# Dense attention regrouped: heads on 32 rows each, four matrix products in different tiles, PSUM split between row maxima and exponentials

## The chip, the cores and the metric

The kernel runs on one core of a Trainium2 chip. The metric is device time in microseconds (us) of one execution; a profile of one execution of the kernel before is at hand.

## The reference, cut to what matters

The program is a chain of twelve sublayers on x, 4 batches of 512 tokens of 128 numbers, float32. Two of the twelve are the dense attentions that the change is about; both have 16 heads of 8 numbers and attend over the 512 tokens of a batch.

```python
# second sublayer ("mqa"): causal, one key and one value head for all 16 query heads
latent = x @ Wc_down                      # 128 -> 64
q = (latent @ Wq_up).reshape(B, T, 16, 8)
k, v = split(latent @ Wkv_up)             # 8 and 8
att = softmax(where(causal, einsum('bthd,bsd->bhts', q, k) / sqrt(8), -inf))
x = x + einsum('bhts,bsd->bthd', att, v).reshape(B, T, 128) @ Wc_proj

# fifth sublayer ("rope"): not causal, own keys and values in each head
q, k, v = proj(Wq, bq), proj(Wk, bk), proj(Wv, bv)      # 16 heads of 8
q, k = apply_rope(q) / sqrt(8), apply_rope(k)
x = x + (softmax(q @ k.T) @ v) @ Wo.T + bo
```

The input of each is the layer-normed x. The order is moe, mqa, moe, chan, rope, chan, swiglu, forget, swiglu, deep, time, deep. The two "deep" sublayers (six layers of windowed attention and feed-forward each) fill the last two thirds of the time and are changed only in where one set of their weights lies.

## The kernel before, in words

Tokens lie along the free dimension and the 128 features on the partitions. Each engine has its own straight program (TensorE, VectorE, ScalarE, GpSimd, and SyncE for loads); they meet by semaphores. A sublayer other than the deep ones runs as a loop over the four batches, and a batch (a "unit") begins on TensorE only when the unit before has added its result to x (`unit_done`, L411 ff.). PSUM has eight banks of 128 x 512 float32.

One unit of dense attention (`dense_pe`, `dense_act`, `dense_dve`):

- Preparation: layer norm (L145, L151, L159 on TensorE, L170 and L174 on ScalarE, L182 to L191 on VectorE), then q, k and v products (L414 to L428), rope on VectorE (L532 to L544), the values laid out (L551, L553).
- L556: VectorE makes 16 masked copies of the keys, `da_kM`, one for each head: all rows but the 8 of that head are zero, so that a product over all 128 rows gives one head's scores. Before the first unit of a sublayer, L511 clears 8320 columns for the values, which are laid out in the same manner, 128 wide with zeros and ones.
- Scores for the maxima: for each tile of 128 queries and each group of 4 heads, four products of 128 x 512 (L444; in the causal sublayer 128 to 512 keys, and one bf16 product L447 that adds the mask) fill four banks; VectorE takes the four row maxima in one reduction (L564). Eight banks hold two such groups.
- L452 turns the 64 columns of maxima, L500 on ScalarE puts them into spare rows of `da_q`, so that the second score product comes out less its maximum.
- Exponentials: for each tile of 128 keys and each head one product (L463, mask L466) into one of four banks, ScalarE takes exp (L506), and a product with the values (L473) adds into bank 6 or 7, which in the end holds both the sums and the denominators.
- End: VectorE copies and inverts the denominators (L569, L571), multiplies (L574), TensorE projects (L477), VectorE adds to x (L578 or L580).

Every matrix product here has float32 operands. In the trace one such product is two records of MATMUL and two of LDWEIGHTS; a bf16 product is one of each.

The chip's tiles can be seen in this kernel in the deep sublayers. L859 makes its four products with 64 columns of weights each, alternately into PSUM rows 0 to 63 and 64 to 127. L797 takes operands from rows 0 to 63 or 64 to 127 and writes PSUM rows in blocks of 32, eight different places in turn; L792, ahead of it, uses all rows and columns.

## Time and profile before

| what | us |
|---|---|
| median of three runs (range) | 6653.96 (6646.73 to 6661.31) |
| the profiled execution, its own time | 6652.98 |
| its span, first to last instruction | 6651.2 |
| mqa sublayer, from one sublayer's last addition to x to its own last | 646.0 |
| rope sublayer, likewise | 832.8 |

The profile page gives busy time by engine over the whole span, and a strip of forty slices; each digit is tenths of full. As the program is a chain of sublayers with different limits, an average over the whole says little about two of them. The two dense sublayers are read as stretches of their own. A TensorE record's length holds the way through the array too, so that consecutive records overlap: the spacing of their starts is what a stream costs, not their length.

### The profile page before, as it was taken

How to read it: one execution, taken by the hardware profiler on the slowest of the kernel's cores; microseconds unless marked ns; L12 is line 12 of the kernel's file. 1: busy time of each engine (PE TensorE's matmuls, PEld its weight loads, DVE VectorE, ACT ScalarE, POOL GpSimd, SP SyncE). 2: the span in 40 equal slices, each digit the busy share in tenths (PEclk: the TensorE clock that was granted, in tenths of full speed). 3: DMA queues.
4: the chain of work that ended last, by engine and by line, in shares of the span. 5: the costliest groups of instructions: out<-in, count | busy, mean ns of one | idle time of the engine just before them, and what ended most of it. 6: DMA issues, size and time to landing. Idle time of an engine off the chain costs nothing.

```text
span 6651.2 us, 145048 instructions
## 1 busy us (share of the span) xinstructions
PE 5355.9 (81%) x64980; PEld 3035.4 (46%) x64980; DVE 3759.9 (57%) x4061; ACT 2357.0 (35%) x2740; POOL 2981.6 (45%) x1264
## 2 busy tenths in 40 slices
PE   5888868898964678888888888856888888888887
PEld 2455533343432344554555545423455555545454
DVE  4222343321224377777777777645777777777774
ACT  1222221122232344444444444423444444444443
POOL 0000000000000277777777777506777777777773
PEclk8888868999965689999999999967998999999998
DMA  1000000000000011111110111100101111111110
GB/s 64 1 0 0 0 0 0 0 0 0 0 0 0 3 26 26 42 26 42 26 42 23 42 26 26 26 34 13 29 23 42 26 42 26 40 26 42 26 26 23
DMA packets 77764, 142.42 MB, mean 21 GB/s; under 512 B 18632, under 2 KB 25488, under 8 KB 75536
## 3 DMA queue, kind: packets, MB, share of 16 engines
q1 hardware_dynamic: 77200, 133.84, 7.8%
q8 instruction: 483, 7.91, 0.5%
q14 instruction: 81, 0.66, 0.0%
HBM read 38.36 MB, written 1.05 MB: 6 GB/s over the span
## 4 chain that ended last, share of the span: by engine, by line
PE 64%; DVE 16%; ACT 7%; issue 7%; POOL 5%; SPq 0%; DVEq 0%; DMA 0%; POOLq 0%; ACTq 0%
PE psum L828 11%; PE psum L444 6%; PE psum L463 6%; PE psum L473 6%; PE psum L890 5%; PE psum L797 4%; PE psum L878 4%; PE psum L859 4%; DVE arena L1093 3%; ACT arena L983 3%; PE psum L811 3%; PE psum L845 3%; DVE arena L1106 2%; DVE arena L1102 2%; POOL arena L1206 2%
## 5 line engine op out<-in xcount | busy, mean ns | idle before, releaser
L1206 POOL TENSOR_TENSOR arena<-arena,minus_half 128x16 f32<-128x16 f32 x384 | 1125.0, 2930 | 1034.0 <-DVE arena L1095 1031.7
L828 PE MATMUL psum<-deep_wqkv,arena 128*128 128x512 f32 x1536 | 877.8, 701 | 432.2 <-DVE arena L1106 424.2
L1221 POOL MEMSET arena<- 128x33 f32 x4 | 0.4, 128 | 2432.0 <-DVE std L1425 2432.0
L1208 POOL TENSOR_TENSOR arena<-arena 128x1024 f32<-128x1024 f32 x384 | 903.4, 2353 | 0.0
L1211 POOL TENSOR_TENSOR arena<-arena 128x1024 f32<-128x1024 f32 x384 | 889.5, 2316 | 30.1
L983 ACT ACTIVATE arena<-psum 128x1024 f32<-128x1024 f32 x384 | 393.4, 1024 | 1040.1 <-PE psum L828 1040.0
L1093 DVE TENSOR_REDUCE arena<-arena 128x16 f32<-128x1024 f32 x384 | 467.0, 1216 | 448.2 <-ACT arena L983 446.6
L828 PEld LDWEIGHTS psum<-deep_wqkv,arena 128*128 128x128 f32 x1536 | 300.8, 212 | 792.2 <-DVE arena L1106 518.7
L845 PEld LDWEIGHTS psum<-w_ident,arena 128*128 128x128 f32 x3072 | 398.7, 153 | 254.9 <-issue 250.6
L1085 DVE TENSOR_TENSOR arena<-arena 128x1024 f32<-128x1024 f32 x192 | 491.8, 2561 | 6.6
L1102 DVE TENSOR_TENSOR arena<-psum,arena 128x1024 f32<-128x1024 f32 x384 | 467.2, 1217 | 0.0
L1106 DVE TENSOR_TENSOR arena<-psum,arena 128x1024 f32<-128x1024 f32 x384 | 465.8, 1213 | 0.0
L463 PE MATMUL psum<-arena 128*128 128x512 f32 (+3 forms) x1024 | 455.5, 529 | 10.4 <-ACT arena L500 10.4
L569 DVE COPY arena<-psum 64x512 f32<-64x512 f32 x16 | 11.0, 689 | 784.0 <-PE psum L473 783.8
L473 PE MATMUL psum<-arena 128*128 128x512 f32 (+3 forms) x1024 | 453.2, 527 | 0.0
L444 PE MATMUL psum<-arena 128*128 128x512 f32 (+3 forms) x1024 | 409.9, 550 | 40.7 <-DVE arena L556 37.2
L845 PE MATMUL psum<-w_ident,arena 128*128 128x128 f32 x3072 | 433.5, 288 | 2.4 <-ACT arena L1000 2.4
L506 ACT ACTIVATE arena<-psum 128x512 f32<-128x512 f32 (+3 forms) x512 | 264.9, 517 | 477.3 <-PE psum L463 281.6
L1071 DVE TENSOR_REDUCE arena<-psum 128x16 f32<-128x1024 f32 x192 | 235.1, 1225 | 336.5 <-PE psum L797 336.5
L989 ACT ACTIVATE arena<-psum 128x1024 f32<-128x1024 f32 x384 | 392.0, 1021 | 82.5 <-PE psum L845 82.4
L878 PEld LDWEIGHTS psum<-arena 64*64 64x64 f32 x24576 | 380.5, 136 | 61.0 <-issue 60.4
L878 PE MATMUL psum<-arena 64*64 64x32 f32 x24576 | 402.2, 221 | 2.7 <-issue 2.7
(247 smaller groups left out, 8031.5 us busy)
## 6 DMA issues: line engine op xcount, KB each, us to landing
arena<-arena SPq DMA_DIRECT2D x672, 128.0 KB, 2.4
deep_wqkv<-in_deep_wqkv SPq DMA_DIRECT2D x12, 1536.0 KB, 7.0
deep_wo<-in_deep_wo SPq DMA_DIRECT2D x12, 512.0 KB, 7.5
arena<-arena SPq DMA_DIRECT2D x96, 64.0 KB, 2.0
deep_w<-in_deep_w SPq DMA_DIRECT2D x12, 341.0 KB, 7.6
deep_w<-in_deep_w SPq DMA_DIRECT2D x12, 192.0 KB, 7.5
deep_scales<-in_deep_scales SPq DMA_DIRECT2D x12, 128.0 KB, 8.1
x<-in_x SPq DMA_DIRECT2D x4, 256.0 KB, 3.4
```

The source lines that it names most:

```text
L444: last = nc.tensor.matmul(bank(a + j)[:, 0:keys], da_q[:, h // HALF, qt * P:(qt + 1) * P], da_kM[:, h, 0:keys], start=True, stop=not causal)
L463: last = nc.tensor.matmul(a[:, q0:T], da_kM[:, h, kt * P:(kt + 1) * P], da_q[:, h // HALF, q0:T], start=True, stop=not causal)
L473: nc.tensor.matmul(bank(6 + h // HALF)[:, q0:T], da_Vm[:, h, kt, :], da_PT[:, v % BUFS, q0:T], start=(kt == 0 and h % HALF == 0), stop=(kt ...
L828: last = nc.tensor.matmul(bank(2 + cc), xs[unit_ % 2][:, WIN + t * P:WIN + (t + 1) * P], wqkv[:, half * INNER + cc * 512:half * INNER + (c ...
L845: last = nc.tensor.matmul(turns[:, m * P:(m + 1) * P], roped[:, h:h + 2, :], w.ident[:, :], start=True, stop=True, is_transpose=True)
L878: last = nc.tensor.matmul(bank(odd)[64 * side:64 * side + 64, to:to + WIN], V[64 * r:64 * r + 64, WPT * t + jj, (pair + odd) * 64:(pair + ...
L1093: nc.vector.tensor_reduce(h_sum[a % 2][:, hs], qk_sq[:, hs, :], AX.X, ALU.add).then_inc(de.deep_sq_summed, 1)
L1102: nc.vector.tensor_tensor(turned[:, hs, :].rearrange("p h (a e) -> p h a e", a=2), swapped, sin, ALU.mult).then_inc(de.deep_rope_parts, 1)
L1106: nc.vector.tensor_tensor(roped[:, hs, :], qk_half, under(tabs[:, 2 * half, t, :], shape), ALU.mult).then_inc(de.deep_rope_parts, 1)
L1206: nc.gpsimd.tensor_tensor(h_inv[a % 2][:, hs], h_sum[a % 2][:, hs], minus_half[:, :], ALU.pow).then_inc(de.deep_inv_ready, 1)
L1208: nc.gpsimd.tensor_tensor(dst[:, hs, :], dst[:, hs, :], turned[:, hs, :], ALU.add).then_inc(de.deep_summed, 1)
L1211: nc.gpsimd.tensor_tensor(dst[:, hs, :], dst[:, hs, :], over(h_inv[a % 2][:, hs], [P, LHEADS, LD]), ALU.mult).then_inc(de.deep_roped, 1)
```

## The change: what it does

Both dense sublayers are written anew.

- A head has 32 rows instead of 8 of 128: row 0 to 7 its numbers, row 8 a one in the keys and (later) minus the maximum in the queries, the rest zero. Four heads make a set, four sets a batch. The widening is made by products with fixed 0/1 matrices (`ra_widen`, four for q and four for k in each batch) or with padded weights (`mqa_q`, `mqa_k`); ScalarE copies each result out. The values are 32 wide with a one at column 8, so that their product gives the denominator in row 8. The masked key copies, the clearing of the value area and the two-half layout go.
- The preparation of all four batches comes first, one batch's layer norm beside the one before; then all score work; then all ends. The per-batch loop is gone: the instructions are written out.
- Score products take 32 rows, the four heads of a set on four different row blocks. The products for the maxima go one head at a time into three single banks (0 to 2) and VectorE reduces each by itself. The products for the exponentials go two heads at a time into a pair of banks (3 and 4, or 5 and 6), and ScalarE takes exp of a pair in one instruction. The value products write 32 rows of bank 7 each, four heads side by side; ScalarE copies bank 7 out after the four key tiles of a set.
- In one step TensorE issues for one tile: a maxima product, two exponential products, a maxima product, the same again, and then the value products of the tile before. The maxima are those of batch b and the exponentials those of batch b - 1, in five rounds; the first has no exponentials and the last no maxima. The maxima are turned once for each set, and VectorE adds them into `da_Q`.
- At the end of a sublayer each batch has eight products of 128 x 512 with fixed matrices (`dense_sum_pe`), which gather the sums and the denominators from the widened rows, then a reciprocal, a product, the projection (`dense_out_pe`) and the addition to x.
- The second set of deep weights moves into the arena, over space that the dense sublayers use, and its first load waits until the first deep sublayer begins. The loads at the start lose those 2.6 MB and gain some 1.2 MB of wider matrices.

The added code, cut to its core (preparation, bias, rope and end functions left out):

```diff
--- before.py
+++ after.py
-ARENA = 34400
-EARLY = 20700
+ARENA = 39860
+ODD_LAYER = 34430
+EARLY = 30724
...
-        deep_kept = [{n: sb(f"{n}_{h}", list(d[n].shape[1:])) for n in layered} for h in range(2)]
-        deep_w = [namedtuple("Layer", [n[5:] for n in layered])(*deep_kept[h].values()) for h in range(2)]
...
+        top[0] = ODD_LAYER
+        deep_kept = [{n: sb(n + "_0", list(d[n].shape[1:])) for n in layered}, {n: new(*d[n].shape[2:]) for n in layered}]
+        deep_w = [namedtuple("Layer", [n[5:] for n in layered])(*deep_kept[h].values()) for h in range(2)]
...
+        SETS = 4
+        GROUPS = SETS * TILES
+        KEY_ORDER = (2, 3, 0, 1)
+        WIDE = SETS * P
+        da_Q = new(NB * SETS, T)
+        da_K = new(NB * SETS, T)
+        da_V = new(NB * TILES, WIDE)
+        da_PT = new(2 * SETS, T)
+        mx = new(SETS * TILES, P)
...
+        def bank_use(q, x_, j):
+            return (17 * q - 1 if q else 0) + 4 * x_ + j + (1 if q and x_ else 0)
+        def bank_use_max(q):
+            return 17 * (q + 1) - 1 + (4 if q + 1 < NB * SETS else 0)
...
+        def dense_wide_pe(pe, e, lhs, src, N):
+            if e >= 2:
+                pe.wait_ge(da.wide_kept, N.wide_kept + e - 1)
+            nc.tensor.matmul(bank(4 + e % 2), lhs, src, start=True, stop=True).then_inc(da.wide_ready, 1)
+        def dense_scores_pe(pe, causal, b, s, x_, j, N):
+            v, keys = bank_use(b * SETS + s, x_, j), (x_ + 1) * P if causal else T
+            if v >= 3:
+                pe.wait_ge(da.banks_free, N.banks_free + v - 2)
+            apart(pe)
+            r32, to = slice(32 * j, 32 * j + 32), bank(v % 3)
+            last = nc.tensor.matmul(to[:, 0:keys], da_Q[r32, b * SETS + s, x_ * P:(x_ + 1) * P],
+                                    keys_of(causal, b, s)[r32, 0:keys], start=True, stop=not causal)
             if causal:
+                last = nc.tensor.matmul(to[:, x_ * P:keys], identb[:, :], later_key_q[:, :], start=False, stop=True)
+            last.then_inc(da.scores_ready, 1)
+        def dense_max_pe(pe, q, N):
+            v = bank_use_max(q)
+            pe.wait_ge(da.banks_free, N.banks_free + max(v - 2, bank_use(q, TILES - 1, 3) + 1))
+            for qt in range(TILES):
+                last = nc.tensor.matmul(bank(v % 3)[:, qt * P:(qt + 1) * P], mx[:, q % SETS * TILES + qt, :], w.ident[:, :],
+                                        start=True, stop=True)
+            last.then_inc(da.max_turned, 1)
+        def dense_keys_pe(pe, causal, b, s, kt, half, N):
+            group = GROUPS * b + TILES * s + kt
+            q0 = kt * P if causal else 0
+            kk = keys_of(causal, b, s)
+            m = 2 * group + half
+            if kt == 0 and half == 0:
+                pe.wait_ge(da.banks_free, N.banks_free + bank_use_max(b * SETS + s) + 1)
+            if m >= 2:
+                pe.wait_ge(da.probs_ready, N.probs_ready + m - 1)
+            apart(pe)
+            for at in range(2):
+                j = KEY_ORDER[2 * half + at]
+                r32, to = slice(32 * j, 32 * j + 32), bank(3 + 2 * (m % 2) + at)
+                last = nc.tensor.matmul(to[:, q0:T], kk[r32, kt * P:(kt + 1) * P], da_Q[r32, b * SETS + s, q0:T],
+                                        start=True, stop=not causal)
+            if causal:
+                for at in range(2):
+                    last = nc.tensor.matmul(bank(3 + 2 * (m % 2) + at)[:, q0:q0 + P], identb[:, :], later_key_k[:, :], start=False,
+                                            stop=True)
+            last.then_inc(da.keys_ready, 1)
+        def dense_mix_pe(pe, causal, group, N):
+            b, s, kt = group // GROUPS, group // TILES % SETS, group % TILES
+            q0 = kt * P if causal else 0
+            pe.wait_ge(da.probs_ready, N.probs_ready + 2 * group + 2)
+            if kt == 0 and group >= TILES:
+                pe.wait_ge(da.y_kept, N.y_kept + group // TILES)
+            apart(pe)
+            for at in range(SETS):
+                j = KEY_ORDER[at]
+                c0 = 0 if causal else s * P + 32 * j
+                last = nc.tensor.matmul(bank(7)[32 * j:32 * j + 32, q0:T], da_V[:, b * TILES + kt, c0:c0 + 32],
+                                        da_PT[:, group % 2 * SETS + at, q0:T], start=(kt == 0), stop=(kt == TILES - 1),
+                                        skip_group_check=True)
+            last.then_inc(da.pv_done, 1)
+        def dense_attend_pe(pe, causal, N):
+            made = 5 * NB if causal else 8 * NB
+            pe.wait_ge(da.wide_kept, N.wide_kept + made)
+            pe.wait_ge(da.v_kept, N.v_kept + (NB if causal else NB * TILES))
+            for body in range(NB + 1):
+                for s in range(SETS):
+                    for x_ in range(TILES):
+                        group = GROUPS * (body - 1) + TILES * s + x_
+                        for half in range(2):
+                            if body < NB:
+                                dense_scores_pe(pe, causal, body, s, x_, 2 * half, N)
+                            if body >= 1:
+                                dense_keys_pe(pe, causal, body - 1, s, x_, half, N)
+                            if body < NB:
+                                dense_scores_pe(pe, causal, body, s, x_, 2 * half + 1, N)
+                        q = body * SETS + s - 1
+                        if x_ == 0 and 0 <= q < NB * SETS:
+                            dense_max_pe(pe, q, N)
+                        if group >= 1:
+                            dense_mix_pe(pe, causal, group - 1, N)
+            dense_mix_pe(pe, causal, GROUPS * NB - 1, N)
+        def dense_sum_pe(pe, b, N):
+            pe.wait_ge(da.y_kept, N.y_kept + SETS * (b + 1))
+            if b >= 2:
+                pe.wait_ge(da.y_ready, N.y_ready + b - 1)
+            for to, lhs, done in ((2 * (b % 2), w.da_den, da.den_ready), (2 * (b % 2) + 1, w.da_own, da.ysum_ready)):
+                for s in range(SETS):
+                    last = nc.tensor.matmul(bank(to), lhs[:, s, :], da_Q[:, b * SETS + s, :], start=(s == 0), stop=(s == SETS - 1))
+                last.then_inc(done, 1)
+        def dense_exp_act(act, causal, group, N):
+            q0 = group % TILES * P if causal else 0
+            for half in range(2):
+                m = 2 * group + half
+                if half == 0 and group >= 2:
+                    act.wait_ge(da.pv_done, N.pv_done + group - 1)
+                act.wait_ge(da.keys_ready, N.keys_ready + m + 1)
+                at = group % 2 * SETS + 2 * half
+                nc.scalar.activation(da_PT[:, at:at + 2, q0:T], banks(3 + 2 * (m % 2), 2)[:, :, q0:T],
+                                     ACT.Exp).then_inc(da.probs_ready, 1)
+        def dense_y_act(act, q, N):
+            act.wait_ge(da.pv_done, N.pv_done + TILES * (q + 1))
+            nc.scalar.activation(da_Q[:, q, :], bank(7), ACT.Copy).then_inc(da.y_kept, 1)
+        def dense_max_dve(dve, causal, b, s, x_, j, N):
+            q = b * SETS + s
+            v, keys = bank_use(q, x_, j), (x_ + 1) * P if causal else T
+            dve.wait_ge(da.scores_ready, N.scores_ready + 4 * (TILES * q + x_) + j + 1)
+            if x_ == 0 and j == 0 and q >= SETS:
+                dve.wait_ge(da.max_turned, N.max_turned + q - SETS + 1)
+            at = 32 * j + HD8
+            nc.vector.tensor_reduce(mx[:, s * TILES + x_, at:at + 1], bank(v % 3)[:, 0:keys], AX.X, ALU.max,
+                                    negate=True).then_inc(da.banks_free, 1)
+        def dense_lay_max_dve(dve, q, N):
+            v = bank_use_max(q)
+            dve.wait_ge(da.max_turned, N.max_turned + q + 1)
+            nc.vector.tensor_tensor(da_Q[:, q, :], bank(v % 3), da_Q[:, q, :], ALU.add).then_inc(da.banks_free, 1)
...
                     load_layer(sp, c, 0)
+                    sp.wait_ge(g.unit_done, first_deep)
                     load_layer(sp, c, 1)
...
-                    per_unit(pe, dense_pe, u, n, k, kind == "mqa", other)
+                    dense_pe(pe, u, n, kind == "mqa", dense_base[kind])
...
+    widen, den = np.zeros((P, 4, P), f), np.zeros((P, 4, P), f)
+    for i in p:
+        s, j, e = i // 32, i // 8 % 4, i % 8
+        widen[i, s, 32 * j + e] = 1
+        den[32 * j + 8, s, i] = 1
+    c["ra_widen"], c["da_own"], c["da_den"] = widen, widen.transpose(2, 1, 0).copy(), den
+    c["da_one"] = (p % 32 == 8).astype(f)[:, None]
```

## Rows read from the trace of the kernel before

**Rows 1.** The page: TensorE's busy time, and its granted clock in 40 slices.
```profile
PE 5355.9 (81%) x64980; PEld 3035.4 (46%) x64980; DVE 3759.9 (57%) x4061; ACT 2357.0 (35%) x2740; POOL 2981.6 (45%) x1264
...
PEclk8888868999965689999999999967998999999998
```

**Rows 2.** Stretches (mqa, rope, one unit of each): busy by engine, PEclk, DMA.
```profile
160.20:806.20 646.00, 563.57 (x2218) 332.00 (x2218) 172.99 (x193) 140.08 (x296) 0.00 (x0) 0.88 0.00 0
1008.50:1841.30 832.80, 741.51 (x1714) 332.74 (x1712) 245.34 (x225) 182.08 (x292) 0.00 (x0) 0.92 0.00 0
328.50:487.60 159.10, 141.13 (x553) 84.56 (x554) 41.16 (x47) 35.02 (x74) 0.00 (x0) 0.88 0.00 0
1226.30:1431.10 204.80, 184.36 (x428) 82.66 (x428) 59.26 (x56) 45.51 (x73) 0.00 (x0) 0.93 0.00 0
```

**Rows 3.** Groups by shape in the rope unit: count | busy, mean ns | idle before, releaser.
```profile
L463 PE MATMUL psum<-arena 128*128 128x512 f32 x128 | 66.8, 607 | 1.3 <-ACT arena L500 1.3
...
L444 PE MATMUL psum<-arena 128*128 128x512 f32 x128 | 57.2, 610 | 6.4 <-DVE arena L556 6.4
...
L564 DVE TENSOR_REDUCE arena<-psum 128x4 f32<-128x2048 f32 x16 | 36.7, 2292 | 17.5 <-PE psum L444 17.5
```

**Rows 4.** Timeline, rope unit: start, length of the merged run, engine and line.
```profile
1248.63 57.24 PE L444 MATMUL psum<-arena 128*128 128x512 f32 x128 [6.44 <-DVE arena L556]
...
1305.90 2.29 DVE L564 TENSOR_REDUCE arena<-psum 128x4 f32<-128x2048 f32 x1 [1.14 <-PE psum L444]
1308.25 1.16 PE L452 MATMUL psum<-w_ident,arena 128*128 128x128 f32 x8 [2.38 <-DVE arena L564]
1309.45 0.59 ACT L500 ACTIVATE arena<-psum 64x512 f32<-64x512 f32 x1 [69.14 <-PE psum L452]
...
1418.08 1.02 PE L473 MATMUL psum<-arena 128*128 128x512 f32 x2
1418.94 1.02 PE L463 MATMUL psum<-arena 128*128 128x512 f32 x2
...
1424.02 3.35 DVE L571 RECIPROCAL arena<-arena 128x512 f32<-128x512 f32 x1
```

**Rows 5.** Timeline of TensorE, mqa: the start of a unit, then scores with masks.
```profile
349.23 0.80 PE L444 MATMUL psum<-arena 128*128 128x128 f32 x2 [2.87 <-DVE arena L556]
...
199.50 0.65 PE L444 MATMUL psum<-arena 128*128 128x256 f32 x2
199.99 0.22 PE L447 MATMUL psum<-arena,identb 128*128 128x128 bf16 x1
200.04 0.65 PE L444 MATMUL psum<-arena 128*128 128x256 f32 x2
```

**Rows 6.** Timeline of TensorE in a deep sublayer, where tiles are used.
```profile
3004.19 0.20 PEld L859 LDWEIGHTS psum<-deep_wqkv,arena 128*64 128x64 f32 x4
3004.19 1.94 PE L859 MATMUL psum<-deep_wqkv,arena 128*64 128x512 f32 x8
3004.67 0.14 PEld L859 LDWEIGHTS psum<-deep_wqkv,arena 128*64 128x64 f32 x2 [0.28 <-issue]
3005.10 0.14 PEld L859 LDWEIGHTS psum<-deep_wqkv,arena 128*64 128x64 f32 x2 [0.29 <-issue]
3006.06 0.12 PEld L792 LDWEIGHTS psum<-maskb,identb 128*128 128x128 bf16 x2 [0.81 <-issue]
...
3006.60 1.33 PE L797 MATMUL psum<-arena 64*32 64x64 f32 x110
3009.15 0.41 PE L797 MATMUL psum<-arena 64*32 64x64 f32 x18 [1.22 <-issue]
```

**Rows 7.** Groups of the whole trace or of the mqa unit: reductions and exponentials.
```profile
L564 DVE TENSOR_REDUCE arena<-psum 128x4 f32<-128x512 f32 x4 | 2.7, 686 | 4.2 <-PE psum L447 4.2
...
L983 ACT ACTIVATE arena<-psum 128x1024 f32<-128x1024 f32 x384 | 393.4, 1024 | 1040.1 <-PE psum L828 1040.0
```

**Rows 8.** Timeline of ScalarE: the end of the loads at the start.
```profile
34.17 1.28 ACT L1367 ACT_TABLE_LOAD   x1 [34.17 <-DMA w_rope<-in_rope]
```

More of the change, by code:

```diff
@@ new lines, in program @@
+        da_xn = [new(T) for _ in range(2)]
+        da_lat = new(T)
+        top[0] = early + 2 * T
+        da_bias, da_cos, da_turn = [new(T) for _ in range(2)], [new(T) for _ in range(2)], [new(T) for _ in range(2)]
+        top[0] = early
+        da_inv, da_y = [new(T) for _ in range(2)], [new(T) for _ in range(2)]
+        def bank_use(q, x_, j):
+            return (17 * q - 1 if q else 0) + 4 * x_ + j + (1 if q and x_ else 0)
+        def bank_use_max(q):
+            return 17 * (q + 1) - 1 + (4 if q + 1 < NB * SETS else 0)
@@ new lines, in dense_rot_pe, with dense_values_pe @@
+        def dense_rot_pe(pe, b, N):
+            for m in range(2):
+                pe.wait_ge(da.bias_kept, N.bias_kept + 2 * b + m + 1)
+                nc.tensor.matmul(bank(2 + m), w.rot8[:, :], da_bias[m], start=True, stop=True).then_inc(da.rot_ready, 1)
+        def dense_values_pe(pe, b, kt, N):
+            i = TILES * b + kt
+            if i >= 2:
+                pe.wait_ge(da.v_kept, N.v_kept + i - 1)
+            nc.tensor.matmul(bank(6 + i % 2), da_xn[b % 2][:, kt * P:(kt + 1) * P], w.ra_wv[:, :], start=True,
+                             stop=True).then_inc(da.v_ready, 1)
@@ new lines, in dense_out_pe, with dense_pe @@
+        def dense_out_pe(pe, u, b, causal, N):
+            pe.wait_ge(da.y_ready, N.y_ready + b + 1)
+            if b >= 2:
+                pe.wait_ge(g.unit_done, u + b - 1)
+            nc.tensor.matmul(bank(4 + b % 2), (w.mqa_proj if causal else w.ra_wo)[:, :], da_y[b % 2], start=True,
+                             stop=True).then_inc(da.out_ready, 1)
+        def dense_pe(pe, u, n, causal, N):
+            dense_prepare_pe(pe, u, n, causal, N)
+            dense_attend_pe(pe, causal, N)
+            pe.wait_ge(da.probs_ready, N.probs_ready + 2 * GROUPS * NB)
+            dense_sum_pe(pe, 0, N)
+            for b in range(NB):
+                if b + 1 < NB:
+                    dense_sum_pe(pe, b + 1, N)
+                dense_out_pe(pe, u, b, causal, N)
@@ L1253, in program @@
         last_unit = units
+        dense_base, done = {}, da._make([0] * len(da))
+        for kind in sublayers:
+            if kind in dense_counts:
+                dense_base[kind] = done
+                done = da._make([a + b for a, b in zip(done, dense_counts[kind])])
+        first_deep = [u for kind, u, n, k, other in plan if kind == "deep"][0]
         n_fixed = len(fixed)
@@ L1327, in _ @@
             for kind, u, n, k, other in plan:
-                if kind == "deep":
+                if kind in ("mqa", "rope"):
+                    dense_pool(pool, u, n, dense_base[kind])
+                elif kind == "deep":
                     deep_pool(pool, call, u + NB)
@@ L1379, in _ @@
                 elif kind in ("mqa", "rope"):
[L1380 removed]
+                    dense_act(act, n, kind == "mqa", dense_base[kind])
                 elif kind == "time":
@@ L1493, in laid_out @@
         L["ra_b" + n] = rows(v["L1_attn_bv"]) if n == "v" else col(v["L1_attn_b" + n])
+    L["ra_wv"] = wide(L["ra_wv"]).reshape(P, 4 * P)
+    ones = np.tile(np.arange(32) == HD8, HEADS8).astype(np.float32)
+    L["ra_bv"] = rows(np.where(ones, ones, wide(v["L1_attn_bv"][None]).reshape(-1)))
     L["fo_wf"] = np.repeat(v["L2_attn_Wf"].T, HD8, axis=1)
```

386 lines of the change are left out of this document (190 added, 196 removed).

## The prediction

> **What bounds the kernel now.** I read the page first. TensorE is busy 81% of the span and its granted clock is mostly full [rows 1]; over a chain of sublayers that is only a hint, so I cut out the two dense sublayers. In both TensorE is busy nearly 90% of the stretch (563.6 of 646.0 us, 741.5 of 832.8), VectorE and ScalarE under 30% [rows 2]. The groups of one rope unit say with what: L444 and L463, 128 records of 128x512 each, hold 124 us of TensorE, L473 has as many records again, and ahead of them it was idle for a few us only [rows 3], in a unit of 204.8 [rows 2]. L564 waits for L444, not the other way round [rows 3]. One float32 product of 512 columns costs the spacing of starts, 1418.94 - 1418.08 = 0.86 us, 0.43 a record [rows 4]; 192 of them are 165 us of a rope unit. So the dense sublayers are bound by TensorE's streaming, and only what shortens the streams, or runs several at once, helps.
>
> **Can tiles run at once here?** L859 answers: its eight records of 512 columns, in two column tiles, load their weights in pairs at 3004.19, 3004.67 and 3005.10, and the whole took 1.94 us [rows 6], where eight records one after another are 8 x 0.43 = 3.4. Two tiles stream side by side at full rate. L797, in eight tiles, ran 110 records in 1.33 us [rows 6]: 12 ns each, where 64 columns at 0.43 us for 512 are 53 ns; at least four at once, over two row blocks. What the trace doesn't show is four row blocks, nor records with a semaphore wait between them.
>
> **A change of tile shape** has a price. L859's last pair starts at about 3005.53 (0.43 after 3005.10), its stream ends at 3005.96, and L792, of another shape, starts at 3006.06: a gap of 0.10. The first pair was 3004.67 - 3004.19 = 0.48 apart from the second, 0.05 over the usual 0.43, since no load was hidden. I take 0.15 for each change. Bounds: 0.10, the gap alone; 0.30, if the new shape waits until results are out (a pair of records lasts 1.02 where its stream is 0.86, so 0.16 on top) and the load is bare. A mask without a change of shape costs 200.04 - 199.50 - 0.43 = 0.11 [rows 5].
>
> **The rope sublayer.** A step (one set, one tile) has four maxima products, four exponential products, four value products. Within a row block a product's two records follow each other. Products separated by waits I let overlap by one record only: a new product starts when the last record of the one before has started, since TensorE starts in order. Then half a step is product, pair, product = 3 x 0.43 = 1.29 between starts; two halves and the last record 3.0; change of shape, four value products side by side 0.86, change back: 3.0 + 0.15 + 0.86 + 0.15 = 4.2 us. The same work was 12 x 0.86 = 10.3 before.
> Does anything else bind? VectorE's four single-bank reductions are 4 x 0.69 = 2.7 [rows 7]. A bank's cycle is reduction 0.69, 0.06 to TensorE, product 1.02, 0.04 back (1308.25 after 1305.90 + 2.29, and 1309.45 after 1308.25 + 1.16 [rows 4]) = 1.8, for three banks 0.6 a product. ScalarE's two exponentials are 2 x 1.02 [rows 7] and a quarter of a 0.6 copy = 2.2. All below 4.2.
> Turning the maxima is eight records of 128 columns, 1.16 [rows 4], once in four steps. Rounds 2 to 4: 48 x 4.2 + 12 x 1.15 = 215. The first round, maxima only, goes at VectorE's pace: 2.6 and a quarter of (addition 0.69, wait for the turning 0.6) = 2.95, x 16 = 47. The last goes at ScalarE's and TensorE's, 2.8 x 16 = 45. Together 307.
> Preparation: a batch has some 20 products of 0.86 (q, k, two turns, four values, eight widenings, the norm's), 17 us, and about 2 of waits; four and a first norm of 10: 86. Before, it was 1248.63 - 1226.3 = 22.3 in each unit [rows 2, 4]: little is won. The ends: 32 products of 0.86 are 27.5, then reciprocal 3.35 [rows 4], product, projection, addition: 35. Sum 86 + 307 + 35 = 428 against 832.8: **405 less**.
>
> **The mqa sublayer.** Mean width is 2.5 of 4 tiles, so a product streams 0.54. Here every maxima product is followed by a mask in another shape, so nothing overlaps: 0.54 + two changes 0.30 + 0.06 for the mask = 0.9, x 256 = 229. Exponential pairs: 0.54 + 0.30 + two masks 0.11 = 0.95, x 128 = 121. Value products 0.54 + 0.30, x 64 = 53. Turnings 16 x 1.3 = 21. Together 424; VectorE and ScalarE are far below. Preparation 58 (20.7 in each unit before, 349.23 - 328.5 [rows 2, 5]; now one batch beside the other), ends 35: 517 against 646.0: **129 less**.
>
> **The rest.** The loads at the start end at 34.17 [rows 8]; three more of them and wider ones: 3 us more, all on the path. GpSimd's clearing of the maxima lies beside the preparation. The odd layer's load now begins with the deep sublayer and is wanted a layer later; ahead of it on SyncE's queue nothing waits, and behind it the first moves of values wait for a first tile of work anyway: nothing. If that cover failed it would be the 7 us of a load, once. The deep sublayers are otherwise untouched.
>
> Sum: 6651.2 - 405 - 129 + 3 = 6120 of span, 1.8 around it; the profiled execution (6653.0) is 1 us from the median. **6125.**
>
> Of four row tiles the Trainium skill (TensorE: Matmul & The Clock Gate, Measured speedup vs the span model) states 3.07 times, not 4; no run here shows it yet. By that figure, as an estimate, four value products would take 1.12 instead of 0.86 and the sum would be 6150. The same skill (TensorEngine Tiling (Array Packing), Key Properties) says that a change of tiling mode drains the array; the gap of 0.10 in rows 6 agrees.
>
> **The rivals.**
> A, as above, 6125; the price of a change moves it: some 14 x 64 in mqa, 2 x 64 and the turnings in rope, 1090 in all, so 0.10 gives 6070 and 0.30 gives 6290. Chance 0.60.
> B, no overlap across waits: each separately awaited product of rope runs by itself, a step is 6 x 0.86 + 0.86 + 0.30 = 6.3, and 48 steps cost 100 more: 6230. For it: the trace shows tiles side by side only in runs without waits. Against: matmuls behind a met wait (L473) keep the spacing of 0.43. Chance 0.17.
> C, the evacuation binds: three single banks for the maxima make VectorE and TensorE take turns. By rows, the product for a step's fourth head can't start before the first is reduced, 1.8 after; a delay only if tiles overlap better than I let them, and then a step is 3.9 to 4.3, within 10 us of A; with changes of shape at 0.10 also, 6065. The Trainium skill (TensorEngine Tiling, PSUM Bottleneck) warns that tiling speeds up the products and not the evacuation; 2.7 against 4.2 says it isn't reached. Chance 0.10.
> D, the clock stays at 1.2 GHz in the dense sublayers, as it did at the start of a mqa unit (0.80 for two records of 128 columns at 349.23 against 0.65 for 256 later [rows 5]). Every stream doubles, some +270 in mqa and +245 in rope: 6640, no change. Against: 0.88 and 0.92 were granted in these stretches [rows 2], and TensorE will still have work without a break. Chance 0.05.
> E, slower: products in the four row blocks run one after another. A rope step is 12 x 0.86 + 0.6 = 10.9, the sublayer 820 against 833; mqa's pairs and value products double and fourfold, 690 against 646: 6685. It decides from the point where a step takes over 10.8 us. L859 and L797 speak against it [rows 6]. The same side is reached if a change of shape costs over 0.64 us, 0.49 more than taken, 1090 times; the largest that rows allow is 0.30. Chance 0.05 for both.
> What is left, 0.03, is that it is faster by other amounts.
>
> **The numbers.** The likeliest case is A. From 6040, below C, to 6290 (A with dear changes, B) lies 0.8; outside are D, E and the edges. A measurement can tell some 0.2%, 13 us, from no change. Faster by more: A, B, C and the rest, 0.92 with part of D; within it 0.03; slower 0.05.
>
> **What would show it.** In the trace after, rope's steps 4.2 to 4.5 us apart in rounds 2 to 4 (6.3: B; over 10: E), starts of a pair a few ns apart, mqa's maxima products 0.9 apart on average, the granted clock over 0.85 in both, the sublayers about 517 and 428 long, the deep ones unchanged. I am wrong if TensorE is not the engine without idle time in rounds 2 to 4, or if the deep part moves.

## The result, and the profile after

The changed kernel takes 6414 us (median of 4 runs, 6399 to 6445) against 6657 (4 runs, 6647 to 6661) on the same chip: ratio 0.964, 95% interval 0.963 to 0.966. It is faster by 243 us, where 530 were forecast, and lies outside the range (6040 to 6290). The profiled execution took 6399, its span is 6397.3.

Its page, TensorE's busy time and granted clock in 40 slices, as in [rows 1]:

```profile
PE 5269.4 (82%) x65388; PEld 2847.2 (45%) x65388; DVE 3734.7 (58%) x4283; ACT 2321.0 (36%) x2524; POOL 2982.7 (47%) x1265
...
PEclk8555576789656899999999999858999999999998
```

The last line is the granted clock, the share of TensorE's full clock that it was allowed, in tenths. Its first slices are what is new: 5 where there were 8. Stretches of the same trace, columns as in [rows 2]: the mqa sublayer, the rope sublayer, rounds 2 to 4 of mqa (most of them), then rope's maxima-only round and its rounds 2 to 4:

```profile
163.90:961.20 797.30, 789.53 (x2400) 309.76 (x2400) 163.25 (x300) 120.05 (x178) 1.80 (x1) 0.56 0.00 0
1165.30:1600.20 434.90, 425.69 (x1936) 165.71 (x1936) 227.01 (x336) 166.86 (x195) 1.80 (x1) 0.90 0.00 1
...
332.00:790.00 458.00, 458.00 (x1351) 172.53 (x1350) 86.96 (x172) 61.69 (x89) 0.00 (x0) 0.50 0.00 0
1251.00:1323.00 72.00, 72.00 (x171) 37.36 (x171) 43.02 (x67) 2.05 (x2) 0.00 (x0) 0.50 0.00 1
1330.00:1520.00 190.00, 190.00 (x1159) 62.94 (x1158) 121.23 (x188) 91.90 (x100) 0.00 (x0) 1.00 0.00 1
```

Rope went from 832.8 [rows 2] to 434.9, as forecast (428). Mqa, forecast at 517, went from 646.0 to 797.3: it became slower, and in the middle of it TensorE is busy without a gap for 458 us at a granted clock of 0.50, which is the level of 1.2 GHz; before, the sublayer had 0.88 [rows 2]. By parts, mqa is now 66 us of preparation, 107 of maxima alone (round 1, 230.1 to 337.5), 543 of rounds 2 to 4 (to 880.3), and 81 of the last round and the ends. Where the two spans differ, in order of time: the loads end at 35.96 instead of 34.17 (+1.8); mqa, cut in both from the end of moe's last addition (162.07 and 163.88), +153; between the dense sublayers +2; rope -398; all behind it -13. Sum -254. The last is hardly an effect of the change: the part behind rope took 4809.9 us before and 4797.1 after, and in the runs below, where it is the same program as after, between 4805 and 4818: executions of that one program spread over 21 us.

Mqa's maxima products at the slow clock, timeline of TensorE (L514 the product of 32 rows, L517 its mask of 128 rows):

```profile
255.31 0.79 PE L514 MATMUL psum<-arena 32*128 32x128 f32 x2
256.03 0.29 PE L517 MATMUL psum<-arena,identb 128*128 128x128 bf16 x1
256.25 0.79 PE L514 MATMUL psum<-arena 32*128 32x128 f32 x2
```

Each maxima product is followed by a mask of another shape, and nothing overlaps it: 0.94 us for one head's 128 keys. One rope step of rounds 2 to 4 looks quite different:

```profile
1450.12 0.69 PE L514 MATMUL psum<-arena 32*128 32x512 f32 x1
1450.12 0.70 PE L543 MATMUL psum<-arena 32*128 32x512 f32 x2
1450.14 1.10 PE L514 MATMUL psum<-arena 32*128 32x512 f32 x2
...
1451.10 1.00 PE L543 MATMUL psum<-arena 32*128 32x512 f32 x2
...
1452.11 1.09 PE L514 MATMUL psum<-arena 32*128 32x512 f32 x2
1453.14 1.06 PE L561 MATMUL psum<-arena 128*32 128x512 f32 x8
1454.13 0.69 PE L514 MATMUL psum<-arena 32*128 32x512 f32 x1
...
1451.28 2.66 DVE L727 TENSOR_REDUCE arena<-psum 128x1 f32<-128x512 f32 x4 [1.35 <-PE psum L514]
```

Products of four heads start within 0.02 us of each other, although a semaphore wait stands ahead of each maxima product and each pair; a second group starts about 1 us later, then the fourth maxima product alone (1452.11), then the four value products side by side (1453.14). The last row is VectorE's, four reductions of 0.66 each: the first ends at about 1451.95, and the fourth maxima product, which needs that bank, starts at 1452.11. The step is 4.01 us.

### The profile page after: what moved, and what is told of

The parts are those of the page before. It is cut to its first block, busy times and chain, and to the rows that moved or that the text cites. A ratio compares the mean times of both kernels' runs of the same rounds, so it can differ in the third digit from the quotient of the medians.

```text
span 6397.3 us, 145495 instructions
## 1 busy us (share of the span) xinstructions
PE 5269.4 (82%) x65388; PEld 2847.2 (45%) x65388; DVE 3734.7 (58%) x4283; ACT 2321.0 (36%) x2524; POOL 2982.7 (47%) x1265
## 4 chain that ended last, share of the span: by engine, by line
PE 56%; issue 19%; DVE 13%; ACT 6%; POOL 6%; SPq 0%; DMA 0%; DVEq 0%; POOLq 0%
PE psum L1020 11%; PE psum L514 5%; PE psum L1082 5%; PE psum L989 5%; PE psum L1070 5%; PE psum L1051 4%; DVE arena L1285 4%; ACT arena L1175 3%; PE psum L1003 3%; PE psum L1037 3%; DVE arena L1298 3%; DVE arena L1294 3%; PE psum L543 2%; POOL arena L1398 2%; PE psum L984 2%
## 5 line engine op out<-in xcount | busy, mean ns | idle before, releaser
L1175 ACT ACTIVATE arena<-psum 128x1024 f32<-128x1024 f32 x384 | 393.5, 1025 | 1043.4 <-PE psum L1020 1043.4
L1020 PE MATMUL psum<-deep_wqkv,arena 128*128 128x512 f32 x768 | 452.8, 720 | 247.8 <-DVE arena L1298 239.8
L727 DVE TENSOR_REDUCE arena<-psum 128x1 f32<-128x512 f32 (+3 forms) x512 | 291.0, 589 | 599.7 <-PE psum L517 502.5
L514 PE MATMUL psum<-arena 32*128 32x512 f32 (+3 forms) x1024 | 578.6, 780 | 2.4 <-ACT arena L646 1.7
L1020 PE MATMUL psum<-arena 128*128 128x512 f32 x768 | 428.4, 685 | 184.0 <-DVE arena L1298 184.0
L656 ACT ACTIVATE arena<-psum 128x1024 f32<-128x1024 f32 (+3 forms) x256 | 214.4, 863 | 735.9 <-PE psum L547 571.6
L1181 ACT ACTIVATE arena<-psum 128x1024 f32<-128x1024 f32 x384 | 391.7, 1020 | 81.5 <-PE psum L1037 81.2
L1192 ACT ACTIVATE arena<-psum 128x1024 f32<-128x1024 f32 x192 | 196.6, 1024 | 450.7 <-PE psum L1003 450.7
```

Source lines behind the costliest of these rows:

```text
L514: last = nc.tensor.matmul(to[:, 0:keys], da_Q[r32, b * SETS + s, x_ * P:(x_ + 1) * P], keys_of(causal, b, s)[r32, 0:keys], start=True, sto ...
L1020: last = nc.tensor.matmul(bank(2 + cc), xs[unit_ % 2][:, WIN + t * P:WIN + (t + 1) * P], wqkv[:, half * INNER + cc * 512:half * INNER + (c ...
L1175: nc.scalar.activation(qk_sq[:, HALVES[half], :], qk_half, ACT.Square).then_inc(de.deep_qk_squared, 1)
```

## The experiments

Three theories for mqa's clock went on record before the first four of these runs. T1: it follows how much of the array streams, and one 32-row product at a time is too little. T2: the many changes of tile shape hold it down. T3: the sublayer enters at the slow clock and nothing lifts it. Sublayer times are cut as above; line numbers move by a few in the variants. A kernel marked timing only leaves out or replaces a part of the computation, as said there. Those and e1_no_max_mask are one execution each, the others four.

**Without the mask behind the maxima products** (an upper bound serves as well as the maximum):

```
-                                    keys_of(causal, b, s)[r32, 0:keys], start=True, stop=not causal)
-            if causal:
-                last = nc.tensor.matmul(to[:, x_ * P:keys], identb[:, :], later_key_q[:, :], start=False, stop=True)
+                                    keys_of(causal, b, s)[r32, 0:keys], start=True, stop=True)
```

> The mask product after every maxima product of the mqa sublayer is gone (the maximum is then taken over the whole diagonal tile, an upper bound, which divides out). Three theories of why the granted clock was half in that sublayer. T1: what counts is how much of the array streams; a 32-row product that a full-height mask cuts off from its neighbours uses a quarter of it, and four that overlap use all of it. T2: the changes of tile shape (some 14 a step) keep it down. T3: the sublayer comes out of its preparation at half and nothing in it lifts the clock. T1: the maxima products now overlap, the clock is full through rounds 2 to 4, the mqa sublayer takes about 320 us instead of 797, the kernel about 5940. T2: 6 changes a step are left of 14; clock perhaps mixed, the sublayer 400 to 600. T3: clock still half, only the masks and their changes are saved, sublayer about 660, kernel about 6280.

6062 us; mqa 445.5. The whole sublayer, and rounds 2 to 4:

```profile
164.45:609.98 445.53, 436.00 (x2144) 197.94 (x2144) 157.12 (x300) 120.00 (x178) 1.80 (x1) 0.78 0.00 1
...
330.00:520.00 190.00, 190.00 (x1266) 81.73 (x1264) 85.31 (x179) 66.31 (x96) 0.00 (x0) 0.96 0.00 1
```

256 small masks gone, and 352 us with them. The clock is 0.96 in most of rounds 2 to 4, so T3 falls: the preparation is the same and something lifts it. This run doesn't decide between T1 and T2: the sublayer is 125 longer than I wrote for T1 (320), and 445.5 lies in T2's 400 to 600. The first round stays at 0.50, and a step of rounds 2 to 4 takes 4.8 us (230.9 for 48).

**Maxima products of full height, masks of 32 rows** (timing only):

```
-            r32, to = slice(32 * j, 32 * j + 32), bank(v % 3)
+            r32, to = slice(0, P) if causal else slice(32 * j, 32 * j + 32), bank(v % 3)
...
-                last = nc.tensor.matmul(to[:, x_ * P:keys], identb[:, :], later_key_q[:, :], start=False, stop=True)
+                last = nc.tensor.matmul(to[:, x_ * P:keys], identb[32 * j:32 * j + 32, :],
+                                        later_key_q[32 * j:32 * j + 32, :], start=False, stop=True)
```

> Timing only: in mqa the maxima products contract over all 128 rows instead of 32 (the scores of four heads added up), and the mask behind each contracts over 32 rows only. The number of changes of tile shape, the widths streamed and the order of waits stay as in the changed kernel; only the long streams are now of full height. T1: clock full in the attend part of mqa, maxima products about 0.9 us apart, the sublayer about 520 us, the kernel about 6120. T2 and T3: clock still half, sublayer about 790, kernel about 6410.

6112 us; mqa 495.9. The sublayer, rounds 2 to 4, and some of its maxima products:

```profile
164.85:660.79 495.94, 488.14 (x2400) 213.26 (x2400) 162.36 (x301) 119.96 (x178) 1.80 (x1) 0.92 0.00 1
330.00:580.00 250.00, 250.00 (x1460) 108.59 (x1459) 90.97 (x182) 67.70 (x97) 0.00 (x0) 1.00 0.00 1
```

```profile
423.84 0.44 PE L514 MATMUL psum<-arena 128*128 128x128 f32 x2
424.21 0.22 PE L517 MATMUL psum<-arena,identb 32*128 32x128 bf16 x1
424.36 0.49 PE L514 MATMUL psum<-arena 128*128 128x128 f32 x2
```

The same count of products, with the same widths and waits, still one after another, and 301 us less. Two heights differ, the product's and the mask's, and with them the changes of shape: by the order of issue, 9 a step in rounds 2 to 4 instead of 13, since a narrow mask and the pair behind it share a shape, and so do the pair's masks and the next maxima product. By the price measured below, 0.09 us a change, the 192 changes fewer are some 17 of the 301 at full clock (an estimate). T2 isn't thereby excluded, as 9 could be few enough; the next run settles it. This is also, nearly, the mqa sublayer that the prediction had costed: 517 at full clock.

**Rope with all 32-row products in one row block** (timing only: head 0's rows stand in for every head):

```
-            r32, to = slice(32 * j, 32 * j + 32), bank(v % 3)
+            r32, to = slice(32 * j, 32 * j + 32) if causal else slice(0, 32), bank(v % 3)
```

and the same for the exponential products.

> Timing only: in the rope sublayer all maxima and exponential products contract over row block 0 (head 0's rows for every head), so that they run one after another, as mqa's do, but with no mask and no change of shape between them. T1: one 32-row product at a time streams, so the clock falls to half in rounds 2 to 4 as well; a step is 16 us, the sublayer about 1140 us instead of 435, the kernel about 7100. T2 or T3: the clock stays full, a step is 8 x 0.86 + 0.86 + 0.3 = 8.1 us, the sublayer about 655, the kernel about 6640.

7149 us; rope 1129. The mqa and the rope sublayer, rounds 2 to 4 of rope and of mqa, and TensorE's timeline in rope:

```profile
164.75:1001.29 836.54, 828.75 (x2400) 321.69 (x2400) 163.22 (x300) 120.15 (x178) 1.80 (x1) 0.52 0.00 0
1207.95:2337.02 1129.07, 1121.41 (x1936) 408.49 (x1936) 238.94 (x336) 173.77 (x195) 1.80 (x1) 0.56 0.00 0
...
1405.00:2158.00 753.00, 753.00 (x1230) 268.88 (x1229) 140.42 (x203) 104.30 (x107) 0.00 (x0) 0.52 0.00 0
347.50:890.30 542.80, 542.80 (x1612) 204.97 (x1612) 101.97 (x203) 74.16 (x107) 0.00 (x0) 0.50 0.00 0
```

```profile
1700.28 3.62 PE L543 MATMUL psum<-arena 32*128 32x512 f32 x4
1703.69 3.62 PE L514 MATMUL psum<-arena 32*128 32x512 f32 x4
```

Four records in 3.41 us, 0.85 each instead of 0.43: the clock halves in rope too (0.52), in rounds that ran at 1.00, with no mask and no change of shape among these products, and with the same work for TensorE in all but the row block. T2 would have left it full (655): it falls, and T1 holds as far as these two runs go. So products one after another are slow twice here: nothing overlaps, and the clock is half. The first row is mqa of the same run, untouched, and 39 us longer than in the changed kernel's own trace. Its rounds 2 to 4 took 542.8 us in both executions; the 39 lie in the preparation (9) and in the last round, which stayed at half here (76 instead of 47).

**Masks of 32 rows behind 32-row products** (timing only): the second change of e7_wide_max_narrow_mask, to the mask, alone.

> Timing only: the maxima products of mqa stay 32 rows high as in the changed kernel, and the mask behind each stays too, but contracts over the same 32 rows, not 128. If it is the height of the mask that kept the products apart (T1): products in four row blocks overlap, the clock is full in rounds 2 to 4, the sublayer is about 450 us, as without that mask (445.5), the kernel about 6065. If a mask with its float32 to bfloat16 change keeps them apart whatever its height: the clock stays half, the sublayer about 750, the kernel about 6370.

6156 us; mqa 533.7. The clock goes up and down within rounds 2 to 4:

```profile
164.30:697.95 533.65, 524.35 (x2400) 235.79 (x2400) 157.22 (x300) 119.99 (x178) 1.80 (x1) 0.66 0.00 1
305.00:380.00 75.00, 75.00 (x305) 29.80 (x306) 18.35 (x38) 14.08 (x21) 0.00 (x0) 0.50 0.00 1
405.00:430.00 25.00, 25.00 (x188) 11.12 (x185) 11.22 (x23) 7.80 (x12) 0.00 (x0) 1.00 0.01 1
505.00:580.00 75.00, 75.00 (x305) 29.56 (x304) 18.12 (x38) 13.85 (x20) 0.00 (x0) 0.50 0.00 1
```

Between the two expectations (450 and 750). The mask's height is most of it (797 to 534): behind a narrow mask products of different row blocks do start together (341.27 and 341.28 us at the half level, 409.10 and 409.11 at the full one). But the same loop runs at either level for long, so this overlap alone doesn't keep the clock full as T1 said. What tips it no run here shows.

**Both of full height** (timing only): the first change of e7_wide_max_narrow_mask alone, so that maxima products and masks run over 128 rows.

> Timing only: as e7_wide_max_narrow_mask (maxima products of mqa over all 128 rows), but the mask behind each is of full height again, so two changes of tile shape go from each of 256 maxima products, 512 in all; the clock stays full, as it did there (mqa took 495.9 us). Price of a change as I took it, 0.15 us: 77 us less, the sublayer 419, the kernel about 6035. At the lower bound of 0.10: 51 less, 445 and 6061. At 0.30: 154 less, 342 and 5958. If a change costs nothing in itself: no difference, 496 and 6112.

6074 us; mqa 461.5 against 495.9. Against the changed kernel only the maxima products' height differs here (and with it the changes of shape, 6 a step), and the clock is full. Most of rounds 2 to 4, then its timeline to set beside the one above:

```profile
330.00:580.00 250.00, 250.00 (x1572) 117.09 (x1576) 86.92 (x172) 77.94 (x112) 0.00 (x0) 1.00 0.00 1
...
423.18 0.44 PE L514 MATMUL psum<-arena 128*128 128x128 f32 x2
423.45 0.22 PE L517 MATMUL psum<-arena,identb 128*128 128x128 bf16 x1
423.51 1.11 PE L525 MATMUL psum<-w_ident,arena 128*128 128x128 f32 x8
```

Product to mask takes 0.27 without a change of shape and 0.37 with one (424.21 - 423.84); mask to next 0.06 and 0.15. So a change adds 0.09 to 0.10 at full clock to the spacing without one. My 512 changes fewer were miscounted: in rounds 2 to 4 it is 3 a step (9 against 6) and in the first round 8, 272 in all. Rounds 2 to 4 took 265.1 us against 278.2, 13.1 for 144 changes, again 0.09. The other 21 us are the first round (48.0 against 69.2), in part because it ran at the full clock sooner.

The prediction's 0.15 was counted from the bare stream, and by that measure it is nearer: two changes and the mask take 424.36 - 423.84 - 0.21 = 0.31 where 0.36 were forecast, and around rope's value products the two changes are 1453.14 - 1452.11 - 0.86 = 0.17 and 1454.13 - 1453.14 - 0.86 = 0.13, the 0.30 of the forecast.

**All masks off TensorE.** Nothing stands behind a maxima product, as in e1_no_max_mask, and GpSimd multiplies the diagonal tile of each pair of exponentials by 0 and 1, and the value products wait for it:

```
+                for m in range(2 * GROUPS * NB):
+                    group, half = m // 2, m % 2
+                    at, q0 = group % 2 * SETS + 2 * half, group % TILES * P
+                    pool.wait_ge(da.probs_ready, N.probs_ready + m + 1)
+                    to = da_PT[:, at:at + 2, q0:q0 + P]
+                    nc.gpsimd.tensor_tensor(to, to, under(own_or_later[:, :], [P, 2, P]), ALU.mult).then_inc(da.masked, 1)
```

> All masks of mqa leave TensorE: no mask behind the maxima products (an upper bound serves), and GpSimd multiplies the diagonal 128x128 of each pair of exponentials by a table of 0 and 1 before the value products. What is left of mqa's attend part is rope's, with half the width. T1 and T2: clock full in rounds 2 to 4, a step about 2.4 us, the sublayer about 285 us instead of 797, the kernel about 5900. T3: clock half, sublayer about 460, kernel about 6080. If GpSimd, with two multiplications a step, takes over 1.2 us for each, it sets the step instead.

5959 us (4 runs, 5956 to 5964), ratio to the kernel before 0.896, 95% interval 0.894 to 0.897. It beats both kernels. Its mqa sublayer, the first round, rounds 2 to 4, and rope:

```profile
165.15:515.09 349.94, 323.95 (x1888) 162.98 (x1888) 153.95 (x301) 112.97 (x178) 93.22 (x129) 0.82 0.00 1
230.00:285.00 55.00, 52.65 (x160) 34.04 (x160) 31.94 (x67) 1.97 (x2) 0.00 (x0) 0.50 0.00 1
305.00:430.00 125.00, 115.74 (x1016) 58.80 (x1012) 77.47 (x168) 55.56 (x88) 55.77 (x78) 1.00 0.01 1
717.68:1150.25 432.57, 423.31 (x1936) 164.71 (x1936) 226.45 (x337) 166.93 (x195) 1.80 (x1) 0.91 0.00 1
```

349.9 where 285 were expected: the first round, still at 0.50, took 52 (231.3 to 283.5), and a step of rounds 2 to 4, turnings and all, takes 3.3 (48 steps from 283.5 to 439.9) instead of 2.4 and the turnings. GpSimd's multiplications took 0.73 each, two a step, and don't set it.

**What sets a rope step?** Theory A of the prediction: TensorE's own starts and streams. Theory C: three banks; the fourth maxima product waits for the first's reduction, and the value products queue behind it. First, the value products ahead of the fourth maxima product, on top of the kernel above:

```
+                            if half == 1 and group >= 1:
+                                dense_mix_pe(pe, causal, group - 1, N)
                             if body < NB:
                                 dense_scores_pe(pe, causal, body, s, x_, 2 * half + 1, N)
...
-                        if group >= 1:
-                            dense_mix_pe(pe, causal, group - 1, N)
```

> e4_masks_on_gpsimd (5959 us) with the four value products of a step issued ahead of its fourth maxima product instead of behind it, in both dense sublayers. Theory C (the cycle of three banks sets the step: the fourth product waits for the reduction of the first, and the value products queue behind that wait): the wait is now covered by the value products; a rope step goes from 4.0 to 3.0-3.3 us (VectorE's four reductions and gaps 2.9, TensorE's streams 2.6 + two changes 0.3), mqa's mean step from 3.1 to about 2.6; 48 of each: 35 to 50 and 20 to 30 less, the kernel 5880 to 5905. Rival: TensorE's own streams and starts set the step (theory A of the prediction), the order doesn't matter: within 10 us of 5959. Another: the value products now wait for the second exponential of the step before and hold up the fourth maxima product: slower than 5959.

5999 us (5978 to 6002), 40 slower; rope 443.3 instead of 432.6, mqa 374.7 instead of 349.9, of which 9 lie in its preparation, which the edit leaves alone. One of its rope steps (L557 the value products, L513 maxima, L540 exponentials, L723 VectorE's reductions):

```profile
960.04 1.06 PE L557 MATMUL psum<-arena 128*32 128x512 f32 x8
961.04 0.70 PE L513 MATMUL psum<-arena 32*128 32x512 f32 x2
...
961.06 1.10 PE L513 MATMUL psum<-arena 32*128 32x512 f32 x3
...
962.00 1.02 PE L540 MATMUL psum<-arena 32*128 32x512 f32 x2
963.03 0.66 PE L513 MATMUL psum<-arena 32*128 32x512 f32 x1
...
964.24 1.06 PE L557 MATMUL psum<-arena 128*32 128x512 f32 x8
...
962.19 2.66 DVE L723 TENSOR_REDUCE arena<-psum 128x1 f32<-128x512 f32 x4 [1.54 <-PE psum L513]
```

The value products didn't cover the wait, because the bank cycle now catches another product. The late maxima product streams beside the next step's first group (961.04), and with that group's two maxima products it takes up the three banks. The third maxima product of the step needs the late one's bank: VectorE starts on that at 962.19 and is done with it 0.66 later, and the product starts at 963.03, with the second exponential pair behind it. Before the edit the fourth product waited so, and the second group didn't. A step takes 4.20 instead of 4.01. The last expectation, slower, came true, but not by the wait on the exponentials that it names.

There is a clash of row blocks too. One exponential product of that first group wants the late product's block and starts only when that has streamed (962.00). What is issued behind it isn't held up: the second maxima product comes later in the program, in a free block, and started 0.94 us before it, at 961.06. No record of this step is missing, and 35 of 46 such steps in rounds 2 to 4 show the same.

Second, shorter reductions in the changed kernel (timing only: 128 of rope's 512 columns, the maxima are of those alone):

```
-            nc.vector.tensor_reduce(mx[:, s * TILES + x_, at:at + 1], bank(v % 3)[:, 0:keys], AX.X, ALU.max,
+            nc.vector.tensor_reduce(mx[:, s * TILES + x_, at:at + 1], bank(v % 3)[:, 0:keys if causal else P], AX.X, ALU.max,
```

> Timing only: the changed kernel, but in rope VectorE reduces 128 of a bank's 512 columns (about 0.2 us instead of 0.66), TensorE's work is the same. The rope step of rounds 2 to 4 was 4.02 us. Theory C (three banks: the fourth maxima product waits for the first's reduction, in a row block of its own, and the value products queue behind it): the bank is free before the second group of products starts, the fourth product streams beside them and not alone, a step takes 3.0 to 3.2 us, 48 steps and part of the first round 45 to 55 us less: rope sublayer 380 to 390 instead of 435, kernel about 6360. Theory A (TensorE's own starts and streams): step 4.0, within 10 us of 6414.

6380 us; rope 381.8. The sublayer, its first round, rounds 2 to 4, and VectorE's reductions in most of them, in the changed kernel and here:

```profile
1179.90:1561.71 381.81, 372.56 (x1936) 147.93 (x1936) 129.51 (x337) 166.87 (x195) 1.80 (x1) 0.98 0.00 1
1261.00:1298.00 37.00, 36.37 (x150) 17.77 (x147) 17.42 (x64) 0.81 (x1) 0.00 (x0) 1.00 0.00 1
1298.80:1482.70 183.90, 183.90 (x1233) 67.98 (x1232) 59.64 (x204) 98.68 (x106) 0.00 (x0) 1.00 0.00 1
...
L727 DVE TENSOR_REDUCE arena<-psum 128x1 f32<-128x512 f32 x177 | 114.2, 686 | 64.5 <-PE psum L514 61.0
L727 DVE TENSOR_REDUCE arena<-psum 128x1 f32<-128x128 f32 x188 | 50.4, 289 | 112.2 <-PE psum L514 112.2
```

Then a step:

```profile
1434.91 1.00 PE L543 MATMUL psum<-arena 32*128 32x512 f32 x2
...
1435.53 1.09 PE L514 MATMUL psum<-arena 32*128 32x512 f32 x2
1436.55 1.06 PE L561 MATMUL psum<-arena 128*32 128x512 f32 x8
1437.54 0.69 PE L514 MATMUL psum<-arena 32*128 32x512 f32 x1
```

TensorE's work is the same and a step takes 3.61 us: the fourth product starts 0.62 after the second group, not 1.01. A reduction is 0.40 shorter (0.29 for 0.69) and so is a step. So the reduction is on the path (C), and TensorE's streams alone (A) don't set the step. It isn't the 3.0 to 3.2 expected, since the first product's own 1.1 us and the shorter reduction still keep the fourth waiting until 1435.53. The sublayer gains 53 us, within the 45 to 55 expected: 23 in rounds 2 to 4 and 31 in the first round (68.8 to 38.2), which now ran at 1.00 with the same products of 32 rows, only closer together. The kernel gains only 34: mqa took 810 us in this execution and the part behind rope 4816, both of which the edit leaves alone.

**A filler in the first rounds**, on top of the reordered kernel: one full-height bfloat16 product a step into an unread bank.

> f1 and, in the first round of both dense sublayers (maxima only, granted clock 0.50), one full-height bfloat16 product of 512 columns a step into a bank that nobody reads, 32 in all. T1 (what streams in the array decides): the clock rises in the first round, which takes 45 to 50 us instead of 62 in rope and 40 instead of 58 in mqa, in all 20 to 30 less than f1. If that little more doesn't lift the clock, each filler costs its own 0.43 us and two changes at half clock: 32 x 0.8 = 25 more than f1 at most, nearer 10, since the bank cycle hides part of it.

6024 us, 25 more. Rope's first round:

```profile
830.00:905.00 75.00, 70.49 (x143) 24.72 (x141) 36.14 (x56) 0.00 (x0) 0.00 (x0) 0.51 0.00 1
```

The clock stayed at half, and the two first rounds are 36 us longer than without the fillers (mqa 68.7 against 52.1, rope 89.4 against 70.2), 1.1 for each filler and more than the 0.8 that I took as the most; that the kernel shows only 25 is due to other parts, mqa's preparation for 9. T1 as I had put it promised more than it holds: some full-height work in between doesn't lift the clock.

## Why the prediction was wrong

**Failed: the clock, in mqa.** The step that failed is the refusal of rival D: "against: 0.88 and 0.92 were granted in these stretches, and TensorE will still have work without a break". It had work without a break (458.00 of 458.00 us), and that wasn't enough. The granted clock of before belonged to products of full height; the change makes them a quarter as high and leaves mqa's maxima products one at a time. I gave D 0.05 and only for both sublayers together. Its price was near: 517 + 270 = 787, measured 797, though both terms were some 20 to 30 off, in opposite directions (496 and 301, by e7_wide_max_narrow_mask). Had it been applied to mqa alone, where the prediction itself says that "nothing overlaps", the forecast would have been 6395. The Trainium skill (TensorE: Matmul & The Clock Gate, What's actually happening) says that a monitor of how busy TensorE has been sets the clock. By TensorE's busy time, 458.00 of 458.00 us, that would be the full clock, and the trace shows 0.50; the runs with other heights and row blocks show that busy time isn't the measure.

**Near: mqa's own sum.** At full clock (e7_wide_max_narrow_mask) the sublayer takes 496, forecast 517. That is in part luck. The attend part took 391 where 424 were forecast; with the 192 changes that this run lacks it would be some 408, by the estimate above. Against that its preparation took 72 (58 forecast), and the first round ran at 0.85. In the changed kernel the preparation was 66, the ends 32 (35).

**Right: rope**, 434.9 against 428, by parts: preparation 81 (86), first round 69 (47), rounds 2 to 4 207 (215), last 46 (45), ends 32 (35). The first round is D's mechanism again, at 0.50. A step was forecast at 4.2 and measured 4.01, but for another reason, so that the near hit is in part luck. "Overlap by one record only" was wrong: four products start within 0.02 us across waits, and f1_values_before_fourth_max shows one starting 0.94 before a product issued ahead of it, so that the reason given, "since TensorE starts in order", doesn't hold there either. What then binds is the cycle of three banks, rival C, at its 3.9 to 4.3. The Trainium skill's 3.07 times (same page, Measured speedup vs the span model) is stated for row tiles, and the prediction applied it to the value products, which are column tiles. Here a group of four row-tiled products took 0.97 between starts (1450.12 to 1451.09), which for 4 x 0.86 is 3.5 times; the value products took 0.99 with the change behind them.

**Right: the rest.** Loads +1.8 (3 forecast); the deep sublayers didn't grow, so the odd layer's load cost nothing that shows. Rivals B and E fell: a step isn't 6.3 or 10.9.

Put together, the prediction's sum with mqa at full clock would be met within its range: e7_wide_max_narrow_mask measured 6112 against 6125. The miss of 289 us is in the main the clock in mqa: the 301 between that run and the changed kernel, less some 17 for changes of shape.

What stays open is why e3_narrow_mask runs at both levels, and what mix of streams lifts the clock; the runs only order the cases. Nor was the clock of the preparations explained (0.63 in mqa's, 66 us long; 0.52 in e1_no_max_mask, 78 us long).

## What to carry to other kernels

When products are cut to a quarter of the array's rows, ask for each stretch not whether TensorE is busy but how many row blocks stream at once: anything that must stand between two of them in another shape, a mask above all, serialises them, and with that the clock halved here as well. Put such masks on an engine with room, or leave them out where an upper bound will do; here that turned 243 us of gain into 696. And where several tiles overlap, write down which row block and which bank each product takes, in order of issue, before moving one.

## What was not expected of the hardware

- TensorE busy for 458 of 458 us at a granted clock of 0.50; with the maxima products of full height, 250 of 250 at 1.00 (e2_wide_max_wide_mask).
- Both levels in one loop: 0.50, 1.00, 0.50 over 305 to 580 us of e3_narrow_mask; and one round at 0.50 or 1.00 by how fast another engine freed the banks (rope's first round, e8_short_reductions).
- Matmuls in different row blocks overlap across met semaphore waits, starts 0.02 us apart and 0.97 for a group of four where one takes 0.86. In the same block the next one waits, but one issued behind it, in a free block, started 0.94 us before it.
- A change of tile shape adds 0.09 to 0.10 us at full clock to the spacing of products of one shape.
- The same instructions of mqa took 797, 810 and 837 us in three executions, rounds 2 to 4 of them 542.8 each time; the changed kernel's times spread over 46 us, those of the version without masks on TensorE over 8.
